# New turns of five instruction streams, and a wait of GpSimd for a burst of row scatters moved ahead of the next burst

## What is computed

```python
def ffn(xt):                                   # 8192 tokens, D=128, H=512, E=8, top 2
    scores = softmax(xt @ Wg + bg)
    topk_probs, topk_idx = top_k(scores, 2)
    h = gelu(einsum('nd,edh->enh', xt, W1) + b1, approximate=False)
    eo = einsum('enh,ehd->end', h, W2) + b2
    return einsum('nk,nkd->nd', topk_probs, take(eo, topk_idx))

def attn(x):                                   # 16 heads of 8, each token sees itself and 8 before it
    q, k, v = heads(x @ Wq), heads(x @ Wk), heads(x @ Wv)
    w = softmax(where(valid, q . k_window / (2 * 0.28), -inf))
    return (w . v_window) @ Wo

x = x + 0.5 * ffn(layernorm(x))
x = x + attn(layernorm(x))
x = x + 0.5 * ffn(layernorm(x))
```

## Time and profile before

| | us |
|---|---|
| median of three runs | 1196.98 (1190.79 to 1200.83) |
| the execution that was profiled | 1189.38 |
| its span in the profile | 1187.7 |

### The profile page before, as it was taken

The page is one execution under the profiler, slowest core; times in us unless marked ns, Lnnn a source line. Parts: engine busy times, 40 slices in busy tenths (PEclk is TensorE's granted clock), DMA queues, the critical chain, the costliest instruction groups (busy, mean ns, idle before and its releaser), DMA issues.

```text
span 1187.7 us, 22521 instructions
## 1 busy us (share of the span) xinstructions
PE 883.5 (74%) x6345; PEld 762.6 (64%) x6345; DVE 644.9 (54%) x1309; ACT 500.4 (42%) x1215; POOL 664.4 (56%) x593
## 2 busy tenths in 40 slices
PE   3347857476987789987997848987877857965973
PEld 3336747475866677776766735776776756864863
DVE  5774132431357688896987998696760511210222
ACT  4434424244633363644544415643334433432432
POOL 2574445555578676346765546355765555555552
PEclk9998858788998899998998978999995987988996
DMA  8314212262215411144012121232222224432663
GB/s 271 102 56 96 51 42 50 72 164 61 56 53 125 100 51 37 26 119 98 28 41 49 22 97 56 62 68 61 50 57 57 51 61 103 122 99 71 177 171 115
DMA packets 170489, 96.44 MB, mean 81 GB/s; under 512 B 137713, under 2 KB 154407, under 8 KB 169605
## 3 DMA queue, kind: packets, MB, share of 16 engines
q1 hardware_dynamic: 152420, 59.29, 21.3%
q0 software_dynamic: 17952, 35.71, 9.8%
HBM read 25.77 MB, written 52.35 MB: 66 GB/s over the span
## 4 chain that ended last, share of the span: by engine, by line
PE 33%; DVE 17%; issue 15%; another core or an unknown queue 14%; SPq 6%; DMA 5%; ACT 5%; POOL 4%; ACTq 0%; DVEq 0%; POOLq 0%
PE bank L977 13%; PE bank L960 8%; POOL x_sorted L586 4%; PE bank L875 3%; SPq L469 3%; ACT h_f L764 2%; DMA x_sorted<-hl,slots_all 2%; PE bank L848 2%; DVE prod L1165 2%; PE bank L862 2%; DVE y_sb L1430 2%; DVE prod L1176 2%; DVE prod L1211 1%; DMA y_in<-y_pairs 1%
## 5 line engine op out<-in xcount | busy, mean ns | idle before, releaser
L603 POOL DMA_INDIRECT y_pairs<-y_sb,tile_ids x305 | 351.3, 1152 | 333.9 <-issue 225.0
L764 ACT ACTIVATE h_f<-bank,b_cols 128x256 f32<-128x256 f32 (+1 forms) x736 | 264.9, 439 | 433.5 <-PE bank L960 225.3
L586 POOL DMA_INDIRECT x_sorted<-hl,slots_all x256 | 304.5, 1189 | 174.7 <-issue 87.6
L977 PE MATMUL bank<-w_sb,h_f 128*128 x2440 | 348.1, 297 | 24.1 <-ACT h_f L764 12.7
L977 PEld LDWEIGHTS bank<-w_sb,h_f 128*128 128x128 f32 x2440 | 319.8, 209 | 33.0 <-issue 28.3
L960 PE MATMUL bank<-xsT,w_hl 128*128 128x256 f16 (+1 forms) x2208 | 258.7, 267 | 45.4 <-DMA xsT<-x_sorted 19.3
L960 PEld LDWEIGHTS bank<-xsT,w_hl 128*128 x2208 | 198.8, 103 | 82.1 <-issue 56.2
L1430 DVE TENSOR_TENSOR y_sb<-bank,tile_ids 128x256 f32<-128x256 f32 (+1 forms) x184 | 68.6, 374 | 335.2 <-PE bank L977 161.6
L971 PE MATMUL bank<-b_hl,ones_b 128*128 x184 | 50.1, 272 | 99.4 <-DVE y_sb L1430 76.5
L971 PEld LDWEIGHTS bank<-b_hl,ones_b 128*128 128x128 f16 x184 | 18.7, 102 | 116.5 <-issue 114.0
L1211 DVE TENSOR_TENSOR prod<-score,qkv 128x2304 f32<-128x2304 f32 x32 | 81.5, 2548 | 0.2
(11 more groups left out here) (159 smaller groups left out, 842.3 us busy)
## 6 DMA issues: line engine op xcount, KB each, us to landing
y_in<-y_pairs SPq DMA_DIRECT2D x28, 512.0 KB
x_sorted<-no_rows SPq DMA_DIRECT2D x7, 720.0 KB
y_pairs<-y_sb,tile_ids POOLq DMA_INDIRECT x305
x_sorted<-hl,slots_all POOLq DMA_INDIRECT x256
x_sorted<-no_rows SPq DMA_DIRECT2D x56, 72.0 KB
x_sb<-in_L_attn_x SPq DMA_DIRECT2D x3, 1024.0 KB, 6.3
out<-x_sb SPq DMA_DIRECT2D x3, 1024.0 KB
xsT<-x_sorted SPq DMA_TRANSPOSE x184
```

The lines of the kernel that those rows point to most:

```text
L586: pool.indirect_dma_start(out=x_sorted[p], out_offset=bass.IndirectOffsetOnAxis(ap=slots_all[:, at:at + 1], axis=0), in_=hl[:, c % 2, i // ...
L603: pool.indirect_dma_start(out=y_pairs, out_offset=bass.IndirectOffsetOnAxis(ap=tile_ids[:, t.n % IDS, i, 0:1].bitcast(U32), axis=0), in_=y ...
L764: ins = act.activation(h_part(t, b)[:, k, :], bank[h_banks.uses[u][0]][:, k * t.slots:(k + 1) * t.slots], ACT.Gelu, bias=b1_cols[:, bass.d ...
L977: ins = pe.matmul(into[:, half, :], h_part(t, c // t.per)[:, c % t.per, half * P:(half + 1) * P], w2_flat[:, bass.ds((e * HC + c) * D, D)] ...
```

## The change

Two things change. First, the five strings with the turns are new. Each stream has as many turns on each engine as before, so nothing is computed or moved that was not before; only the order on each engine differs. For POOL the number of tiles whose y stand before each of the eight bursts of a group of pass 1 is:

| group | before | after |
|---|---|---|
| q = 4 | 76 for all eight | 77, 78, 79, 80, 81, 82, 83, 84 |
| q = 5 | 96 for all eight | 96 for all eight |
| q = 6 | 104, 106, 110, 113, 113, 113, 113, 119 | 106, 107, 108, 109, 110, 112, 113, 115 |
| q = 7 | 125, 136, 136, 136, 148, 154, 154, 154 | 126, 131, 133, 135, 139, 146, 153, 155 |

Second, in pass 1 POOL no longer waits behind a burst for its rows to land, but at the head of the next burst of the same group, behind the wait for that chunk of `hl`. The first burst of a group waits for no rows, and for a group's last burst POOL does not wait at all; SP's `rows_sorted` waits for it, as before.

```diff
 POOL_ORDER = (
-    "sssssyysyysyyyyyyyyyyyyyysyyyyysyyyyyyyyyysyyyyyyyyysysysyyyyysyyyyyyyyyysyyysyyyyyyyyyyyyyssssssssyyyyyyyyyy"
-    "yyyyyyyyyyssssssssyyyyyyysyysyyyysyyyssssyyyyyysyyyyyysyyyyyyyyyyysssyyyyyyyyyyyysyyyyyysssyyyyyyyyyyyyyyyyyy"
+    "ssssssyyyysyyyyyyyyyyyyyysyyyyyysyyyyyyyyysyyyyyyyyyysysysyyysyyyyyyyyyyysyyysyyyyyyyyyyyyyysysysysysysysysyy"
+    "yyyyyyyyyyssssssssyyyyyyyyyysysysysyysyysyysyyyyyyyyyyysyyyyysyysyysyyyysyyyyyyysyyyyyysyysyyyyyyyyyyyyyyyyyy"
     "yyyyyyyyyyyy"
 )
 SP_ORDER = (
-    "tttttttttttttttttttttttttttttyyttttyytttttttttttttttttttttttyytttyyttttttttttttttttttyyttttyytttttttttttttttyy"
-    "yytttttttttttttttttttttttttttttttttttttttttttttttttttttyytttyytttyttttttttttttyytttyytttyyytttyytttytttttyyyyy"
+    "ttttttttttttttttttttttttttttyytttyyttttttttttttttttttttttttyyttttyttttttttttttttttttyyttttyyttttttttttttttttyy"
...
```

The strings of PE, DVE and ACT change in the same manner and are left out. In `scatter_rows`:

```diff
                     for i in range(2 * JQ):
                         at = g * (J * 2) + c * (2 * JQ) + i
+                        if f and i % BURST == 0 and (c or i):
+                            before = (c * (2 * JQ) + i) // BURST - 1
+                            at_c, to = before * BURST // (2 * JQ), before * BURST % (2 * JQ) + BURST
+                            pool.wait_ge(rows_scattered[at_c % 2], q * SCATTERS + (at_c // 2 * (2 * JQ) + to) * DMA)
+                            carry_waits(pool)
                         pool.indirect_dma_start(
                             out=x_sorted[p],
                             out_offset=bass.IndirectOffsetOnAxis(ap=slots_all[:, at:at + 1], axis=0),
                             in_=hl[:, c % 2, i // 2, i % 2, :], in_offset=None).then_inc(rows_scattered[c % 2], DMA)
-                        if f and (i + 1) % BURST == 0:
-                            pool.wait_ge(rows_scattered[c % 2], q * SCATTERS + (c // 2 * (2 * JQ) + i + 1) * DMA)
-                            carry_waits(pool)
-                            if i + 1 < 2 * JQ:
-                                yield
+                        if f and (i + 1) % BURST == 0 and i + 1 < 2 * JQ:
+                            yield
                     yield
```

More of the change, by code:

```diff
@@ L67 @@
 PE_ORDER = (
[L68 to L74, removed]
+    "rrrrrrrrrrrrrrrrrrerrrrrrrrreeeeeeeeeeeeeeeeeeeeeeeereeeeeeeeeeeeeereeeeeeeerrreerrrreeeeeeeeeeeeeeeeeeeeeeeee"
+    "reeeeeeeeeeeeeeeeeeeeeeeeeeeeeeeeeeeeeeeeeeeeeeeeeeeeeeeepepeeeepepeeepeeeepepeeepeeeepeepeepeepeeepepepaaaaaa"
+    "pepepaapepeeeeeeeeeeeeeeeaaaeeeeeeeeeeeeeeeeeeeaeeeeeeeeeeeeeeeeeeeeeaaeeaeepepaapappeepepeaapeaapaaaepaaeaape"
+    "aaaeeaaeeaapeppppaapaaraaararerprpeereeereerpeereeaeaeeeeaeeeeeeeeeeeeareeeeeeeeeeeeeeeeeeeeeaeaeeaeeeeppaaapp"
+    "eeeepppeaaeaaeeaaaepeepaapaapaaapepaapaapppaaaaaareaaprrpeerereereerpreeeeeeaaaeereeeeeeeaeeeeeaaaeraaaaaaaaaa"
+    "apapaapaaappppaapaappppppppppaaaeapraaaeeaeeeeereeereerpeeeeereeeeaeeeerarereereaeeeeeeereeeeaeeeeeeeeeeeeeeee"
+    "eeeeeeeeaeaeeaeeaaaeeeeeeeeaaeaaeaaaeeeeaeaaeaeaaaeeeaaeaaeeeeeeeereeeeeererereererererereeeeeeereeeeeeeeeeeee"
     "eeeeeeeeeeeeeeeeeeeeeeeeeeeeeeeeeeeeeeeeeeeeeeeeeeeeeeeeeeeeeeeeeeeeeeeeeeeeeeeeeeeeeeeeeeeeeeeeeeeeeeeeeeeeee"
@@ L78 @@
 DVE_ORDER = (
[L79 to L83, removed]
@@ L84 @@
-    "peeppeeeeeeeeeeeeeeepepeepepeepepeepepeeeeeeeeeeepppp"
+    "rrrrrrrhrrrhrrrhhrrrrrrrrhhrrrrrrhrhrrhrrrrhrrrhhrrrrrererreehehhheeeeerrehrrrrererrrerereeeerrerrerereerrrhhh"
+    "eeppeehheppeppepeeeeeeehheeeeeaeaaaahaeahahhaeaeaeaaeaeahaaeaeaeppaeapeaeaepapeppehaaeaahaaeaaaeaahaaaaaaaeaaa"
+    "aeaarreaaraaaahhaaaaeaeaeaeaeaeaearaeaerareapperrehhapeaeappeppaaahhaeaaeaaaeaahhaaaaaeaaaaaaaaaarraaraaahhaaa"
+    "aeaaeaeaeaaeaeaeaaeaeaearereraaraarahhappaaaaappapphphaaaaaarhaaaahraarrraarrrraraaahhaaaeaaeaaeaeaaeaaearerra"
@@ L85 @@
+    "earerrrehhrrererareaeaeaahhaaaeaeaaaeaahaaaaaeaahaaaaeaarerreeheheerrerrrerrrerehrerhreeeeeeeeehheeehheeeeepep"
+    "eeppeeeeeeeeeeeeeeeeppeepepeepepeeppeeeeeeeeeeeeepppp"
 )
 ACT_ORDER = (
-    "rrrrrrrrrhhrrrrrrrrrrrrrrrherrrrhrrrrrrrrhrheeeeeerreeereerreereereeerheeheerreeeeerrrheeeeeereeeeeeeeeeeeheee"
-    "eeeeeeeeheeeeeeeeeeeeeppeeeppppeepppeepppeeppheeppepepepeepeppephppephppaeeeeeeeeheeeeeeeeeeeeheeeeeeaeeeeeaap"
-    "peeppppppppppeeppaapppeaeappppaappepprrrrehhrrrrrprparpeeereerereerreeeeeereeeeeeeeeeeeaaaeeeehppppppppppppppe"
@@ L93 @@
+    "peeppppppppppeepppaappeeaappeaaeppppprprrrhhrrrrrrrerprapeerererpeeeeeeeeeeeereeeeeeeeeeaaeaeeepphppppeppppeep"
+    "ppppeaaheeppaapppepaapppprrrhrrhrrrreprraprerereerpreeeeeeeeeaaaraahppaapppppphpppppppaappppppppppperrrhrrhrrr"
+    "rpeeeeeaerreeerpeereeeerrreeeeereeeeeeeeeeeeeeaaaeeheeeeeeaaheeeaeaeeeaaeeeerrrhrrrrrreereerherrererreeeeereee"
+    "eeeeeeeeeeeeeheeeeeeeeeheeeeeeeeeeeeeeeeeeeeeeeeeeeeeeeeeeeeeeeeeeeeeeeeeeeeeeeeeeeeeeeeeeeeeeeeeeeeeeee"
 )
 POOL_ORDER = (
-    "sssssyysyysyyyyyyyyyyyyyysyyyyyysyyyyyyyyyysyyyyyyyyysysysyyyyysyyyyyyyyyysyyysyyyyyyyyyyyyyssssssssyyyyyyyyyy"
@@ L96 @@
-    "yyyyyyyyyyssssssssyyyyyyyysyysyyyysyyyssssyyyyyysyyyyyysyyyyyyyyyyysssyyyyyyyyyyyysyyyyyysssyyyyyyyyyyyyyyyyyy"
+    "ssssssyyyysyyyyyyyyyyyyyysyyyyyysyyyyyyyyysyyyyyyyyyysysysyyysyyyyyyyyyyysyyysyyyyyyyyyyyyyyysysysysysysysysyy"
+    "yyyyyyyyyyssssssssyyyyyyyyyysysysysysyysysyysyyyyyyyyyyysyyyyysyysyysyyyysyyyyyyysyyyyyyysyysyyyyyyyyyyyyyyyyy"
     "yyyyyyyyyyyy"
@@ L99 @@
 SP_ORDER = (
-    "tttttttttttttttttttttttttttttyyttttyytttttttttttttttttttttttyytttyyttttttttttttttttttyyttttyytttttttttttttttyy"
-    "yytttttttttttttttttttttttttttttttttttttttttttttttttttttyytttyytttyttttttttttttyytttyytttyyytttyytttytttttyyyyy"
+    "ttttttttttttttttttttttttttttyytttyyttttttttttttttttttttttttyyttttytyttttttttttttttttyyttttttyyttttttttttttttyy"
+    "yytttttttttttttttttttttttttttttttttttttttttttttttyytttttttytyttyttttttytytttttttttyytttyyyttytyttytttttttyyyyy"
     "yyy"
```

5 lines of the change are left out of this document (2 added, 3 removed).

## The result

The changed kernel takes 1225.95 us in the median of four runs (1223.23 to 1228.86), against 1195.37 for the kernel before on the same chip: 1.0243 of it, with a 95% interval of 1.0202 to 1.0283. I had forecast 1188 and a range up to 1214, so this is slower than all that I allowed for.

The account below looks back on a forecast made before the run. No engine was full: DVE bounded 540 to 756 us, PE and DVE were near it to 870, then a chain across engines, with POOL's unbroken chains mattering. Terms -14 + 0 + 1 + 4 + 0 = -9 gave 1188 us, range 1168 to 1214.

Parts of the forecast that it names:

- The reading of the profile: Whole kernel: PE's results reach other engines late while POOL issues without a pause, 1 to 1.5 us after its chain ends.
- the wait that the change moves: POOL at L586, pass 1: 52.5 us in 21 waits for the landing of earlier rows, to fall to 15 to 20.
- The bursts of q=6: Pass 1, 865 to 893 us: spreading them ends DVE's 15.57 us loss at 909.88; -14 us, bounds 0 to -20.
- q=4's bursts: Pass 1, beside attention: one y between each two bursts, 7.2 - 5.9 gives +1 us, bounds -13 and +20.
- The wait: POOL behind 25 of 32 pass 1 bursts: 55 us freed, counted at nothing, worth up to 55 without POOL's idle time.
- The three bursts more inside attention: q=6, 811 to 870 us: a burst can be hidden or hold a result; +4 us, bounds 0 and +15.
- q=7: Bursts spread over tiles 126 to 155: SP's 5.6 us wait against more chain starts; 0, bounds -8 and +8.
- the 10 us of my sign: Check in the profile after: part 6's load would start within 10 us of 1087.
- Pass 0: First 540 us: one q=1 burst before two tiles' y's; other turns at 0, bounded by 9.5 us in both directions.
- my own sign: Prediction wrong altogether if the time before 540 us moves by more than 5 us.
- Rival C: After 870 us: missing pause holds results 2.6 us more per burst; ten of thirteen give +17, 1214 us; chance 0.18.
- Its sign: After 870 us: more DVE and PE waits of 4 to 8 us for "remote" at ends of POOL's chains.

Follow-up runs that it names:

- The ping-pong: Separate kernel, PE and DVE taking turns beside POOL's work: rounds 1.54 us undisturbed, up to 7.00 us beside 16 indirect DMAs without a pause.
- run 20: Not a run number: "another run", then 20 of 34.53 us. That run: the changed kernel with the old turn string on POOL alone, 1.0253 of before.

## Why the prediction was wrong

*The reading of the profile* was right in its mechanism: PE's results come late while POOL issues DMAs without a pause. The ping-pong shows it, and the memsets behind each second DMA agree. Two readings of rows were not right. The 52.5 us in 21 waits are not "the wait that the change moves": they lie between two bursts and stay with the moved wait (49.1 us in 21). And the 15.57 us of DVE in front of 909.88 are for the most part no hold. PE before, around that tile:

```profile
896.80 1.02 PE L816 MATMUL bank<-wg_sb,xnT_r 128*128 128x8 f32 x4 [4.95 <-ACT xnT_r L668]
...
902.81 1.91 PE L977 MATMUL bank<-w_sb,h_f 128*128 x8
...
905.69 1.91 PE L977 MATMUL bank<-w_sb,h_f 128*128 x8
```

PE had waited for ACT, then did routing between the two halves of the tile, whose last matmuls ended at 907.60 by the profile. Only 2.3 of the 15.57 us lie behind that end.

*The bursts of q=6* are a step that failed: -14 us forecast for the end of the long hold at 909.88. The term was mis-sized, since only 2.3 us of that wait had PE's result ready. The wait at that place went, and holds of 11.92, 7.83 and 17.01 us came, inside the attention, where they cost DVE's order as well; the stretch lost 22.0 us. I had spread the bursts and forgotten that what stands between them, y's, is also DMAs. A tile's two y's between two bursts don't cut a chain, they join it.

*q=4's bursts* are the other: +1 forecast, bounds -13 and +20; the stretch alone measured +2.06%, about 24 us. I priced a burst with its y at 0.9 us, by spreading one 7.21 us wait over eight bursts. What came was not a small price for each burst but one hold of 12.94 us behind a chain of eighteen DMAs, and other waits of DVE. The second price, rows that come later because y's stand between them, I did not see at all, though `hl` with its two chunks was in the code; it is why the old wait would not have saved this stretch.

*The wait.* "I count the freed time itself at nothing" held: 1.0009 with the old turns. The 55 us of waits that I let it free were too many: with the new turns and the old wait POOL stands 21.9 us for them in front of a y. But I left the lost pause to a rival with 0.18, although the argument against it, that POOL waits for the next y anyway, fails in just the stretches where y's are ready: there nothing stops POOL.

*The three bursts more inside attention*: +4, bounds 0 and 15. The whole from q=5 on measured +0.94%, 11 us against my -10 for the bursts of q=6 and q=7 and this together; with the pause kept it was +0.2%. The lengthened issues did not matter to the longest hold: in the chain in front of the 17.01 us none was longer than 1.1 us. The rule of the Trainium skill in "DMA: Bandwidth & Descriptors", section "SWDGE vs HWDGE vs iDMA", by which VectorE in its 2-port mode locks GpSimd out of the state that it writes descriptors to, thus had no part in this hold: DVE stood still there.

*q=7* was about right: from tile 120 to the last the lag changes from 30.5 to 36.4 us, and part 6's first load waits for the clearing DMAs and no longer for rows. It starts 38.7 us later than before, not within the 10 us of my sign.

*Pass 0* was put at zero; it gained 0.7% by itself. That the time ahead of 540 us moved by more than 5 us on the way was my own sign that something was missed.

*Rival C* had the right mechanism and the right sign, at 1214. Its sign came as well: behind 935 us DVE has twelve waits for "remote" of 4 to 9 us, where before had seven of that size behind 912 us. But these cost little, as the lag of q=7 shows. C was sized with 2.6 us more per burst, only after 870 us; the longest holds were up to 17 us and lay between 830 and 930 us, on the attention, and q=4's stretch was not in it. My range ended at C's point, when C's price had no upper bound in any row.

## What to carry to other kernels

An engine that issues indirect DMAs can slow down others that share no data with it: look not at its busy share but at its unbroken chains and the time per DMA in them, and at who gets nothing until they end. Work put between two bursts is a pause only if it isn't itself a DMA. Before an idle time is priced as lateness, look when the work that it waits for had ended: here 2.3 of 15.57 us were late, and in another run 20 of 34.53 us were a full ring. Before a wait is moved because "nothing is behind it", ask what it had let through; and price a stall that grows with the length of a chain by the longest chain that the new order can make, not by a mean.
